# A one-core network kernel with routed experts: two indirect scatters in flight instead of one, and expert tiles of the first half that wait only for the first half's scatters and clears

## The chip, the cores and the metric

The kernel runs on one core of one Trainium2 chip. The metric is device time in microseconds (us), the median of a few executions. A profiled execution gives the trace: its span is the time between the first and the last instruction, its own time is a little longer. Engines are called PE (TensorE), DVE (VectorE), ACT (ScalarE), POOL (GpSimd) and SP (SyncE, used here only to issue DMAs).

## What is computed

Two layers on x of shape (4, 2048, 256) in float32, each sublayer with a layer norm ahead and a residual add behind:

```
x = x + L0_attn(norm(x))   # q, k, v projections, short convolution, gated delta rule (16 heads of 16), output projection
x = x + L0_ffn(norm(x))    # 32 experts, each token goes to 8 of them; plus a shared MLP
x = x + L1_attn(norm(x))   # state-space scan over the sequence, 16 states
x = x + L1_ffn(norm(x))    # rows quantized to a 6-bit grid in blocks of 32, then a 256 x 256 product
```

For the change the routed part of `L0_ffn` matters. For each of the 8192 tokens the gate picks 8 experts, and the token's normalized row (256 floats, 1 KB) goes through each of them; the results are summed with weights. That is 65536 routed rows.

## The kernel before

**Three stages.** The sequence is cut into NB = 16 blocks of 512 tokens (128 positions of each of 4 sequences). The first stage is a software pipeline over the blocks (`for j in range(-2, NB + 1)`), with parts called A (input norm, projections), B (the pair matrices of the delta rule and their solve), C (the sequential state update) and P (output projection, routing, shared MLP). P works on block p = j - 1. The second stage is the list of expert tiles; the third, mixed with the second half of the tiles, sums the expert rows per token and does layer 1.

**Halves.** Blocks 0 to 7 are half 0 and blocks 8 to 15 are half 1. Each half has its own DRAM scratch for routed rows (`xs[h]`, seen as scr_xs) and for expert outputs (`ys[h]`, seen as scr_ys). In `xs[h]` each expert owns a region; the rows of a token go to the next free places. `tables(h)` at the end of a half turns the counts into a tile list: NTH = 159 tiles of TILE = 256 rows for a half, NT = 318 in all.

**Scatter.** For block i, P leaves the normalized rows in `xn_r[:, i % 2]` (two buffers) and the destinations in `idx[:, i % 2]`. POOL then issues NC * TOPK = 4 * 8 = 32 indirect DMAs for the block, each of 128 rows of 1 KB. Before each it waits until the one before has landed, so one is under way at any time. There are two semaphores `s_scat`, one for even and one for odd blocks. ACT, before it writes `xn_r` for block p (`route_rows`, seen as line L890, output xn_r), waits until all scatters of block p - 2 have landed, because they read the same buffer.

**Clears.** A tile of 256 rows can reach past the rows that an expert has, so the 256 rows behind each expert's last row are set to zero: `clear_ends(h)` has SP read 32 positions from `ztab` and issue 32 DMAs of 256 KB from `zeros` (line L803). For half 0 this stands in SP's list behind the loads of j = 9; for half 1 behind everything that SP loads for the first stage. 64 more DMAs of fixed place (L795) run at the start; all 128 count on `s_zero`.

**Tiles.** `load_tile(t)` on SP reads a position and an expert number from the table, and issues the load of the rows into `xt` (6 buffers, L825) and of the expert's weights into `wr` (6 buffers, L832). PE transposes the tile (L618), computes gate and up (L629) and down (L637); ACT copies and applies Silu; DVE multiplies (L1721); ACT issues the store to scr_ys (L1116). Ahead of the first load SP waits:

```
sp.wait_ge(s_tab, HALVES)
sp.wait_ge(s_zero, 16 * 2 * HALVES * E)
for n in range(2):
    sp.wait_ge(s_scat[n], 16 * NC * TOPK * NB // 2)
```

that is, for the tables of both halves, all 128 clears and all 512 scatters. The order of work on each engine is written out by hand; each engine carries out its own list in order.

**Gather.** POOL goes on with 512 indirect DMAs that fetch expert rows into `yg` (L869), with two under way: one semaphore for each, used in turn. Those of a half wait until all tiles of that half are stored.

Of the kernel before, what the change touches and what calls it, by code (L numbers as in the profile page):

```python
# [9 lines left out]
NC = TB // CH  # L10
# [68 lines left out]
def network_kernel(nc, x, wproj, wo, wdelta, wb_state, wgate, wc_state, wshared, wexp, wquant, sel,  # L79
# [13 lines left out]
    with ExitStack() as ctx:  # L93
# [204 lines left out]
        s_zero = sem("s_zero")  # L298
        s_xt = [sem(f"s_xt{n}") for n in range(NX)]
# [23 lines left out]
        CHUNKS = NC * NB  # L323
        block = ctx.enter_context(nc.Block())
# [445 lines left out]
        def _(sp):  # L770
# [27 lines left out]
            def clear_ends(h):  # L798

                sp.wait_ge(s_ztab, h + 1)  # L800
                for e in range(E):
                    at = sp.value_load(ztab[0:1, h, e:e + 1], min_val=0, max_val=ROWS - TILE)
                    sp.dma_start(xs[h][bass.ds(at, TILE), :].rearrange("(p r) d -> p (r d)", r=2), zeros[:])\  # L803
                        .then_inc(s_zero, 16)
# [3 lines left out]
            for j in range(1, NB + 1):  # L808
                if j + 3 < NB:
                    load_x(j + 3)  # L810
                load_res(j)
                if j == HB + 1:
                    clear_ends(0)
            clear_ends(1)
            sp.wait_ge(s_tab, HALVES)
            sp.wait_ge(s_zero, 16 * 2 * HALVES * E)
            for n in range(2):
                sp.wait_ge(s_scat[n], 16 * NC * TOPK * NB // 2)
# [16 lines left out]
            for t in range(NT):  # L835
                load_tile(t)
            sp.wait_ge(s_store, 64 * NB)
# [3 lines left out]
        def _(pool):  # L841
            for i in range(NB):
                pool.wait_ge(s_idx, i + 1)
                for c in range(NC):
                    for k in range(TOPK):
                        sent = i // 2 * NC * TOPK + c * TOPK + k
                        if c or k:
                            pool.wait_ge(s_scat[i % 2], 16 * sent)
                        elif i:
                            pool.wait_ge(s_scat[(i - 1) % 2], 16 * ((i - 1) // 2 + 1) * NC * TOPK)  # L850
                        nc.gpsimd.indirect_dma_start(  # L851
                            xs[i // HB][:, :], bass.IndirectOffsetOnAxis(idx[:, i % 2, c, k:k + 1], 0),
                            xn_r[:, i % 2, c, :], None).then_inc(s_scat[i % 2], 16)
# [23 lines left out]
        def _(act):  # L877
# [20 lines left out]
            def route_rows(p):  # L898
                if p >= 2:
                    act.wait_ge(s_scat[p % 2], 16 * NC * TOPK * (p // 2))  # L900
# [1004 lines left out]
```

## Time and profile before

| | |
|---|---|
| median of 3 runs | 3666.69 us (3666.28 to 3671.66) |
| profiled execution, its own time | 3663.13 us |
| its span | 3661.3 us |
| mean granted TensorE clock | 0.825 |
| busy: PE, DVE, ACT, POOL | 2712.2, 2153.5, 1565.2, 1048.7 us |
| issues of indirect scatter (L851) | 512, from 328.5 to 1935.9 us |
| loads of tiles (L825, L832) | 318 each, the first at 1939.1 us |

Times in the rows are us from the start of the span. A row of the time line gives start, length, engine, line, operation, output and inputs, a count and, in brackets, how long the engine was idle before and what ended the idle time. For a DMA issue from POOL the length is the time in which POOL makes the transfer's descriptors, not that of the data. SPq is SP's queue.

### The profile page before, as it was taken

How to read it: one execution, taken by the hardware profiler on the slowest of the kernel's cores; microseconds unless marked ns; L12 is line 12 of the kernel's file. 1: busy time of each engine (PE TensorE's matmuls, PEld its weight loads, DVE VectorE, ACT ScalarE, POOL GpSimd, SP SyncE). 2: the span in 40 equal slices, each digit the busy share in tenths (PEclk: the TensorE clock that was granted, in tenths of full speed). 3: DMA queues.
4: the chain of work that ended last, by engine and by line, in shares of the span. 5: the costliest groups of instructions: out<-in, count | busy, mean ns of one | idle time of the engine just before them, and what ended most of it. 6: DMA issues, size and time to landing. Idle time of an engine off the chain costs nothing.

```text
span 3661.3 us, 109753 instructions
## 1 busy us (share of the span) xinstructions
PE 2712.2 (74%) x46188; PEld 2021.3 (55%) x46188; DVE 2153.5 (59%) x4702; ACT 1565.2 (43%) x2625; POOL 1048.7 (29%) x1028
## 2 busy tenths in 40 slices
PE   4578888888878887875207999997898888643544
PEld 2355555555555655554106888886777777422322
DVE  4878888888888888772201222213444444676675
ACT  4445555545544555511003444444555554432231
POOL 0001333333332333333330000014434431366661
PEclk8768788888888788766558999998999999876666
DMA  6001111111114111111317999997888887333331
GB/s 241 8 9 36 61 56 61 50 64 62 62 62 148 62 61 55 56 56 57 141 52 245 303 305 304 304 311 232 266 280 262 272 266 247 120 94 94 99 93 34
DMA packets 240349, 511.79 MB, mean 140 GB/s; under 512 B 38770, under 2 KB 63860, under 8 KB 239732
## 3 DMA queue, kind: packets, MB, share of 16 engines
q1 hardware_dynamic: 133396, 270.32, 22.6%
q0 software_dynamic: 49152, 134.28, 11.8%
q10 hardware_dynamic: 57312, 100.16, 7.5%
q8 instruction: 368, 6.03, 0.7%
q14 instruction: 121, 0.99, 0.1%
HBM read 303.82 MB, written 200.80 MB: 138 GB/s over the span
## 4 chain that ended last, share of the span: by engine, by line
DMA 55%; PE 28%; issue 7%; DVE 5%; ACT 3%; POOL 1%; SPq 0%; ACTq 0%; POOLq 0%; DVEq 0%
DMA scr_xs<-xn_r,idx 40%; DMA yg<-scr_ys,idx_y 14%; PE ps L629 13%; PE ps L637 6%; PE ps L618 3%; DVE tmp L1426 1%; DVE tu L1429 1%; PE ps L377 1%; DVE conv L1356 1%; PE ps L706 1%; PE ps L669 1%; DMA out<-x 1%; POOL yg L869 1%; PE ps L688 1%; PE ps L364 0%
## 5 line engine op out<-in xcount | busy, mean ns | idle before, releaser
L851 POOL DMA_INDIRECT scr_xs<-xn_r,idx x512 | 528.9, 1033 | 1407.5 <-DMA scr_xs<-xn_r,idx 1062.4
L869 POOL DMA_INDIRECT yg<-scr_ys,idx_y x512 | 519.7, 1015 | 1129.2 <-DMA scr_ys<-y 574.4
L1721 DVE TENSOR_TENSOR h<-sg,ps 128x256 f32<-128x256 f32 x318 | 133.1, 420 | 829.3 <-ACT sg L1106 790.6
L629 PE MATMUL ps<-xT,wr 128*128 128x256 f32 x2544 | 617.1, 386 | 0.0
L629 PEld LDWEIGHTS ps<-xT,wr 128*128 128x128 f32 x2544 | 470.5, 195 | 62.0 <-issue 8.6
L1748 DVE SCALAR_TENSOR_TENSOR x<-yg,wsel,x 128x256 f32<-128x256 f32 x512 | 247.8, 485 | 220.3 <-DMA yg<-scr_ys,idx_y 201.9
L637 PE MATMUL ps<-wr,h 128*128 128x256 f32 x1272 | 334.1, 386 | 57.8 <-DVE h L1721 31.5
L914 ACT ACTIVATE xT<-ps 128x512 f32<-128x512 f32 x382 | 225.3, 594 | 210.5 <-PE ps L618 173.2
L618 PE MATMUL ps<-identity,xt 128*128 128x128 f32 x1272 | 195.7, 277 | 149.9 <-DMA xt<-scr_xs 149.9
L637 PEld LDWEIGHTS ps<-wr,h 128*128 128x128 f32 x1272 | 242.9, 192 | 98.4 <-DVE h L1721 34.0
L914 ACT ACTIVATE y<-ps 128x512 f32<-128x512 f32 x318 | 189.8, 597 | 202.0 <-PE ps L637 186.8
L447 PE MATMUL ps<-sq,w_proj 128*128 128x512 f32 x512 | 271.7, 671 | 3.7 <-ACT raw L958 1.5
L1106 ACT ACTIVATE sg<-ps 128x256 f32<-128x256 f32 x318 | 122.0, 384 | 346.2 <-PE ps L629 322.8
L618 PEld LDWEIGHTS ps<-identity,xt 128*128 128x128 f32 x1272 | 162.4, 144 | 184.3 <-issue 149.4
L1429 DVE TENSOR_TENSOR tu<-tu,tmp 128x60 f32<-128x60 f32 (+14 forms) x480 | 242.9, 506 | 16.5
L377 PE MATMUL ps<-nq,kne 32*32 32x64 f32 x8192 | 197.6, 256 | 71.4 <-issue 40.5
L1426 DVE TENSOR_TENSOR tmp<-tu 128x60 f32<-128x60 f32 (+14 forms) x480 | 241.1, 502 | 13.4
L377 PEld LDWEIGHTS ps<-nq,kne 32*32 32x32 f32 x8192 | 171.4, 132 | 96.9 <-issue 72.8
L1356 DVE SCALAR_TENSOR_TENSOR conv<-raw,conv_w,conv 128x512 f32<-128x512 f32 x288 | 194.9, 744 | 16.0 <-ACT raw L958 16.0
L407 PEld LDWEIGHTS ps<-r_sb,tt 32*32 32x32 f32 x8192 | 135.5, 144 | 106.2 <-issue 72.3
L407 PE MATMUL ps<-r_sb,tt 32*32 32x16 f32 x8192 | 148.6, 207 | 53.9 <-issue 28.7
L393 PEld LDWEIGHTS ps<-s_sb,nq 32*32 32x32 f32 x8192 | 101.3, 118 | 127.7 <-issue 127.5
(244 smaller groups left out, 4216.8 us busy)
## 6 DMA issues: line engine op xcount, KB each, us to landing
wr<-in_wexp SPq DMA_DIRECT2D x318, 384.0 KB
xt<-scr_xs SPq DMA_DIRECT2D x318, 256.0 KB
scr_ys<-y ACTq DMA_DIRECT2D x318, 256.0 KB
scr_xs<-zeros SPq DMA_DIRECT2D x128, 256.0 KB
x_in<-in_x SPq DMA_DIRECT2D x64, 128.0 KB
x_res<-in_x SPq DMA_DIRECT2D x64, 128.0 KB
scr_xs<-xn_r,idx POOLq DMA_INDIRECT x512, 2.6
scr_x<-x_res SPq DMA_DIRECT2D x16, 512.0 KB
```

The costliest lines, as they stand in the source:

```text
L377: last = pe.matmul(ps[quad(q), AP + g, b * 128 + e * 64:b * 128 + e * 64 + 64], kne[quad(q), e, g, at], nq[quad(q), i % 2, :, g, at], star ...
L407: last = pe.matmul(ps[quad(q), RU, D + u * HD:D + (u + 1) * HD], tt[quad(q), c // 2, :, (c % 2) * H + u], r_sb[quad(q), u * HD:(u + 1) * H ...
L447: last = pe.matmul(ps[:, bank, :], w_proj[:, k, w, g * P:(g + 1) * P], xT[:, k, :], start=k == 0, stop=k == G - 1)
L618: last = pe.transpose(ps[:, bank, k * TILE + r * P:k * TILE + (r + 1) * P], xt[:, t % NX, r, k * P:(k + 1) * P], identity[:])
L629: last = pe.matmul(ps[:, bank, half * TILE:(half + 1) * TILE], wr[:, t % NW, at:at + EI], xT2[:, t % NH, k, :], start=k == 0, stop=k == G - 1)
L637: last = pe.matmul(ps[:, bank, r * D:(r + 1) * D], h2[:, t % NH, r * P:(r + 1) * P], wr[:, t % NW, 2 * G * EI:], start=True, stop=True)
L851: nc.gpsimd.indirect_dma_start(xs[i // HB][:, :], bass.IndirectOffsetOnAxis(idx[:, i % 2, c, k:k + 1], 0), xn_r[:, i % 2, c, :], None).the ...
L869: nc.gpsimd.indirect_dma_start(yg[:, n % NG, k, :], None, ys[h][:, :], bass.IndirectOffsetOnAxis(idx_y[:, i, c, k:k + 1], 0))\
L914: nc.scalar.activation(dst, src, func, **more).then_inc(s_xe[bank], 1)
L1426: sT.did(V.tensor_tensor(part, tu[:, :, j + 1:, j:j + 1].broadcast_to([P, 2, rows, j]), tu[:, :, j:j + 1, 0:j].broadcast_to([P, 2, rows, j ...
L1429: sT.did(V.tensor_tensor(tu[:, :, j + 1:, 0:j], tu[:, :, j + 1:, 0:j], part, ALU.add))
L1748: last = V.scalar_tensor_tensor(row, yg[:, n % NG, k, :], wsel[:, i, c, k:k + 1], row, ALU.mult, ALU.add)
```

## The change

Two things are edited. POOL's scatters use the two semaphores by turn within a block (k even or odd) instead of by block, and each scatter waits only for the last but one before it; ACT's wait ahead of `xn_r` still covers all scatters of block p - 2, now on both semaphores. And the clears behind the experts' rows count on a semaphore for each half, `s_ends`. SP's wait ahead of the first tile asks for the scatters of blocks 0 to 7 (SENT * HB on each semaphore) and the clears of half 0, the wait for all scatters and for the clears of half 1 stands ahead of tile 159, and the 32 clears of half 1 are issued one at a time, behind tiles 3, 7, ..., 127. The wait for both tables stays.

```diff
+        SENT = 16 * NC * TOPK // 2
...
-            def clear_ends(h):
-
+            def clear_end(h, e):
                 sp.wait_ge(s_ztab, h + 1)
-                for e in range(E):
-                    at = sp.value_load(ztab[0:1, h, e:e + 1], min_val=0, max_val=ROWS - TILE)
-                    sp.dma_start(xs[h][bass.ds(at, TILE), :].rearrange("(p r) d -> p (r d)", r=2), zeros[:])\
-                        .then_inc(s_zero, 16)
+                at = sp.value_load(ztab[0:1, h, e:e + 1], min_val=0, max_val=ROWS - TILE)
+                sp.dma_start(xs[h][bass.ds(at, TILE), :].rearrange("(p r) d -> p (r d)", r=2), zeros[:])\
+                    .then_inc(s_ends[h], 16)
...
                 if j == HB + 1:
-                    clear_ends(0)
-            clear_ends(1)
+                    for e in range(E):
+                        clear_end(0, e)
             sp.wait_ge(s_tab, HALVES)
-            sp.wait_ge(s_zero, 16 * 2 * HALVES * E)
+            sp.wait_ge(s_zero, 16 * HALVES * E)
+            sp.wait_ge(s_ends[0], 16 * E)
             for n in range(2):
-                sp.wait_ge(s_scat[n], 16 * NC * TOPK * NB // 2)
+                sp.wait_ge(s_scat[n], SENT * HB)
...
             for t in range(NT):
+                if t == NTH:
+                    sp.wait_ge(s_ends[1], 16 * E)
+                    for n in range(2):
+                        sp.wait_ge(s_scat[n], SENT * NB)
                 load_tile(t)
+                if t % 4 == 3 and t < 4 * E:
+                    clear_end(1, t // 4)
...
-                        sent = i // 2 * NC * TOPK + c * TOPK + k
-                        if c or k:
-                            pool.wait_ge(s_scat[i % 2], 16 * sent)
-                        elif i:
-                            pool.wait_ge(s_scat[(i - 1) % 2], 16 * ((i - 1) // 2 + 1) * NC * TOPK)
+                        way, turn = k % 2, (NC * i + c) * TOPK // 2 + k // 2
+                        if turn:
+                            pool.wait_ge(s_scat[way], 16 * turn)
                         nc.gpsimd.indirect_dma_start(
                             xs[i // HB][:, :], bass.IndirectOffsetOnAxis(idx[:, i % 2, c, k:k + 1], 0),
-                            xn_r[:, i % 2, c, :], None).then_inc(s_scat[i % 2], 16)
+                            xn_r[:, i % 2, c, :], None).then_inc(s_scat[way], 16)
...
                 if p >= 2:
-                    act.wait_ge(s_scat[p % 2], 16 * NC * TOPK * (p // 2))
+                    for way in range(2):
+                        act.wait_ge(s_scat[way], SENT * (p - 1))
```

POOL's list at the first block reads so before (ztab, idx, tab are the tables named above; a count behind a row is of equal rows):

```order
L851 DMA scr_xs<-xn_r,idx 147456x256 [waits s_idx]
L851 DMA scr_xs<-xn_r,idx 147456x256 [waits s_scat0] x31
L851 DMA scr_xs<-xn_r,idx 147456x256 [waits s_scat0,s_idx]
L851 DMA scr_xs<-xn_r,idx 147456x256 [waits s_scat1] x31
L851 DMA scr_xs<-xn_r,idx 147456x256 [waits s_scat1,s_idx]
```

and the same place in the changed kernel:

```order
L856 DMA scr_xs<-xn_r,idx 147456x256 [waits s_idx]
L856 DMA scr_xs<-xn_r,idx 147456x256
L856 DMA scr_xs<-xn_r,idx 147456x256 [waits s_scat0]
L856 DMA scr_xs<-xn_r,idx 147456x256 [waits s_scat1]
L856 DMA scr_xs<-xn_r,idx 147456x256 [waits s_scat0]
L856 DMA scr_xs<-xn_r,idx 147456x256 [waits s_scat1]
```

The number and the order of the scatters are the same; the second has no wait any more, and each later one waits for its own semaphore only.

SP's list between the last store of the first stage (L783) and the first tile load reads so before, with the first and the last of 32 clears:

```order
L783 DMA scr_x<-x_res 128x1024 [waits s_x1]
L802 TENSOR_LOAD ztab [waits s_ztab,s_x1st]
L802 ISA x2
L803 ISA
L803 DMA scr_xs<-zeros 128x512
...
L803 DMA scr_xs<-zeros 128x512
L822 TENSOR_LOAD tab [waits s_scat0,s_scat1,s_zero,s_tab]
L822 ISA x2
L825 ISA
L825 DMA xt<-scr_xs 128x512
```

and so in the changed kernel:

```order
L785 DMA scr_x<-x_res 128x1024 [waits s_x1]
L823 TENSOR_LOAD tab [waits s_ends0,s_scat0,s_zero,s_scat1,s_tab,s_x1st]
L823 ISA x2
L826 ISA
L826 DMA xt<-scr_xs 128x512
L830 TENSOR_LOAD tab
L830 ISA x2
L833 ISA
L833 DMA wr<-in_wexp 128x768
```

The 32 clears are gone from this place. Behind the weights of tile 3 one of them now stands ahead of the rows of tile 4, in SP's list of the changed kernel:

```order
L833 DMA wr<-in_wexp 128x768
L802 TENSOR_LOAD ztab [waits s_ztab]
L802 ISA x2
L803 ISA
L803 DMA scr_xs<-zeros 128x512
L823 TENSOR_LOAD tab
L823 ISA x2
L826 ISA
L826 DMA xt<-scr_xs 128x512
```

The same piece of four rows comes behind every fourth tile up to tile 127.

## Rows read from the trace of the kernel before

**Rows 1.** The page: chain that ended last by share, and the costliest group of POOL.

```profile
DMA 55%; PE 28%; issue 7%; DVE 5%; ACT 3%; POOL 1%; SPq 0%; ACTq 0%; POOLq 0%; DVEq 0%
DMA scr_xs<-xn_r,idx 40%; DMA yg<-scr_ys,idx_y 14%; PE ps L629 13%; PE ps L637 6%; PE ps L618 3%; DVE tmp L1426 1%; DVE tu L1429 1%; PE ps L377 1%; DVE conv L1356 1%; PE ps L706 1%; PE ps L669 1%; DMA out<-x 1%; POOL yg L869 1%; PE ps L688 1%; PE ps L364 0%
L851 POOL DMA_INDIRECT scr_xs<-xn_r,idx x512 | 528.9, 1033 | 1407.5 <-DMA scr_xs<-xn_r,idx 1062.4
```

**Rows 2.** Stretches: length, busy by engine with counts, granted clock, DMA share, GB/s.

```profile
core 0: us, PE busy (x) PEld busy (x) DVE busy (x) ACT busy (x) POOL busy (x), PEclk, DMA share, GB/s
900.00:1000.00 100.00, 82.61 (x2591) 58.07 (x2580) 88.48 (x199) 53.01 (x80) 33.01 (x32) 0.85 0.19 60
1800.00:1900.00 100.00, 0.00 (x0) 0.00 (x0) 0.00 (x0) 0.00 (x0) 34.50 (x36) 0.50 0.32 117
2000.00:2400.00 400.00, 400.00 (x2115) 352.56 (x2114) 107.33 (x189) 193.95 (x396) 0.00 (x0) 1.00 0.93 304
```

**Rows 3.** Time line, first and last scatter, last table, SP's clears, first tile.

```profile
328.54 1.83 POOL L851 DMA_INDIRECT scr_xs<-xn_r,idx  x1 [328.08 <-DVE wsel L1562]
1793.89 36.32 SPq L803 DMA_DIRECT2D scr_xs<-zeros  x32
1794.33 0.28 DVE L1614 CAST tab<-ps 8x128 int32<-8x128 f32 x1 [0.47 <-PE ps L515]
1935.89 0.96 POOL L851 DMA_INDIRECT scr_xs<-xn_r,idx  x1 [1.71 <-DMA scr_xs<-xn_r,idx]
1939.09 0.37 SPq L825 DMA_DIRECT2D xt<-scr_xs  x1
```

**Rows 4.** The chain around 1785 us: start, length, what.

```profile
1785.49 2.40 DMA scr_xs<-xn_r,idx
1787.88 0.27 issue
1788.15 2.41 DMA scr_xs<-xn_r,idx
```

**Rows 5.** ACT's waits from 1250 to 1800 us: total, times, longest.

```profile
ACT xn_r L890 <- DMA scr_xs<-xn_r,idx: 67.7, 6, 27.7
```

**Rows 6.** Time line of ACT and DVE, the last two of these waits.

```profile
1662.34 2.07 ACT L890 ACTIVATE xn_r<-x_res,off_route,std_route 128x256 f32<-128x256 f32 x4 [22.34 <-DMA scr_xs<-xn_r,idx]
1760.72 2.07 ACT L890 ACTIVATE xn_r<-x_res,off_route,std_route 128x256 f32<-128x256 f32 x4 [27.67 <-DMA scr_xs<-xn_r,idx]
1771.02 0.69 DVE L1567 TENSOR_TENSOR h_s<-sq_o,ps 128x512 f32<-128x512 f32 x1 [37.79 <-PE ps L487]
```

**Rows 7.** Time line of DVE, last routing step of blocks 1, 7, 9 and 12.

```profile
428.04 1.22 DVE L1562 TENSOR_REDUCE wsel<-sq_o 128x32 f32<-128x1024 f32 x1
1017.02 1.22 DVE L1562 TENSOR_REDUCE wsel<-sq_o 128x32 f32<-128x1024 f32 x1
1223.62 1.22 DVE L1562 TENSOR_REDUCE wsel<-sq_o 128x32 f32<-128x1024 f32 x1
1534.98 1.22 DVE L1562 TENSOR_REDUCE wsel<-sq_o 128x32 f32<-128x1024 f32 x1
```

**Rows 8.** Stretches again, columns as in rows 2.

```profile
2440.00:2460.00 20.00, 20.00 (x108) 17.64 (x107) 2.43 (x6) 9.90 (x20) 5.71 (x6) 1.00 0.99 346
3200.00:3300.00 100.00, 46.58 (x280) 29.18 (x280) 70.16 (x140) 31.86 (x52) 61.20 (x57) 0.71 0.32 96
```

**Rows 9.** Time line of POOL, first and 25th gather.

```profile
2442.68 0.97 POOL L869 DMA_INDIRECT yg<-scr_ys,idx_y  x1 [505.83 <-DMA scr_ys<-y]
2499.35 0.94 POOL L869 DMA_INDIRECT yg<-scr_ys,idx_y  x1 [1.95 <-DMA yg<-scr_ys,idx_y]
```

**Rows 10.** The chain in the tile stage, one tile and the start of the next.

```profile
2100.16 0.44 PE ps L618 x4
2100.60 1.73 PE ps L629 x8
2102.33 0.86 PE ps L637 x4
2103.19 0.44 PE ps L618 x4
```

More of the change, by code:

```diff
@@ L298, in network_kernel @@
         s_zero = sem("s_zero")
+        s_ends = [sem(f"s_ends{h}") for h in range(HALVES)]
         s_xt = [sem(f"s_xt{n}") for n in range(NX)]
```

## The prediction

> **What bounds the kernel now.** I read the chain of work that ended last first. Its shares say where to look: 40% of the span are landings of the indirect scatters, and they are one costly group, 512 issues with 1062.4 us of POOL's idle time ended by the scatter before [rows 1]. So POOL is not busy: it waits for its own last transfer. The chain's pieces show one turn of this: 2.40 us from issue to landing and 0.27 us to the next issue, 2.67 us for a scatter when nothing else runs [rows 4]. From the first issue at 328.54 to the last at 1935.89 there are 511 steps, 3.15 us each [rows 3]; while DVE and PE are busy a turn is longer, 32 in a stretch of 100 us [rows 2].
>
> Next I read the stretches. From 900 to 1000 us the first stage works at full load (DVE 88%, PE 83%), from 1800 to 1900 nothing but POOL works, and from 2000 to 2400 PE is busy all the time at the full clock, with a DMA share of 0.93 [rows 2]. So there are three limits in a row: the first stage at DVE's and PE's own pace, a gap that is scatters alone, and tiles at PE's pace. A tile takes PE 3.03 us, from 2100.16 to 2103.19, without a gap [rows 10].
>
> Two places show what the scatters cost. One is the gap: the last table is written at 1794.61 (1794.33 and 0.28), and the first tile load goes out at 1939.09 [rows 3]. The last scatter lands at about 1938.3 (1935.89 and the 2.40 of [rows 4]), so SP needs 0.8 us after its last wait ends. The other is inside the first stage: ACT waits six times, 67.7 us in total, for scatters of two blocks before, the last two times 22.3 and 27.7 us [rows 5, 6].
>
> **The change part by part.** (1) The gap. The first tile now asks for the tables, the scatters of blocks 0 to 7 and the clears of half 0. All but the second table are long done at 1794: by blocks of 32 turns of about 3.15 us, block 7 has landed at about 1140. So the table ends the wait, and the first load goes out at 1794.61 + 0.8 = 1795.4 on the old clock, against 1939.09: **143.7 us** gained. The 32 clears that stood here took SP 36.3 us [rows 3]; they are hidden now by scatters that go on for another 108 us, and would have delayed the first tile by some 35 us had they stayed, but they are moved away.
>
> (2) The first stage. With two under way a turn is at best half of 2.67 us, 1.33, and not less than POOL's own 1.03 [rows 1, 4]. The trace has no pair of scatters. The nearest rows are the gathers, the same kind of transfer the other way, two at a time: 57 in 100 us beside a busy DVE, 1.75 us each [rows 8]; and beside a DMA load at its limit 24 turns from 2442.68 to 2499.35, 2.36 us each [rows 9]. Upper bound 3.15 (no help at all). I take 1.9, as DVE is busier here. A block of 32 then takes 61 us. The blocks come 98.2 us apart where ACT doesn't stall (428.04 to 1017.02, six blocks [rows 7]), so the backlog is gone and ACT's waits with it. Up to what pace does this hold? 98.2 / 32 = 3.07 us, far above 2.36.
>
> What are the 67.7 us worth? Blocks 9 to 12 come in 311.4 us [rows 7], and three times 98.2 is 294.6: 16.8 us late, and the waits in them are about what is left when the last two (50.0) are taken off the 67.7, that is 17.7. So the early waits pass on in full. The last two fall where A and B have run out; DVE then sits idle 37.8 us for the step that follows the wait [rows 6], so they pass on too. A part of each wait, some 0.4 us, is DVE's step that ends together with it: 67.7 - 6 x 0.4 = **65 us** gained. Bounds: 0 if pairs don't help; 50 if only the last two pass on; 68 at most.
>
> (3) The tile stage of half 0 gets new load. SP issues 32 clears more, 1.135 us each (36.32 / 32, [rows 3]), one for four tiles. Of four tiles' 12.1 us SP's eight issues take, at that same length, 9.1, and the ninth makes 10.2: SP keeps up. Behind a clear stand the rows of the next tile, later by 1.1 us; with six buffers they are asked for some tiles ahead, and PE waits for nothing there today [rows 2]. The DMA engines get 32 x 256 KB = 8.4 MB of clears over 128 tiles (388 us, 22 GB/s) and, at the start, the last block's scatters, 4.2 MB. At 2.2 us a turn these are 70 us with 60 GB/s. Demand is 304 + 22 + 60 = 386 GB/s for 70 us, then 326. From below: from 2440 to 2460, with gathers in pairs beside the tiles, the engines carried 346 GB/s at a share of 0.99 and PE was busy 20.00 of 20.00 us [rows 8]. So 326 costs nothing, and 386 is 40 over: 2.8 MB, 8 us, if the scatters keep their pace; they need not, since each waits for the last but one and so slows down under load; in those 20 us six gathers went out, 3.3 us a turn. I take **4 us** lost. From above: if 304 GB/s were all there is for this mix, 12.6 MB are 41 us.
>
> The Trainium skill ("SBUF — State Buffer", the bandwidth table in "A bandwidth-pool intuition that's wrong") gives about 358 GB/s between HBM and one core. By it the overload of 28 GB/s for 70 us would be 2.0 MB, 5.5 us, and the sum 1.5 us worse than mine; the 346 GB/s in [rows 8] agree with it as far as they go.
>
> (4) The rest. The wait ahead of tile 159 comes some 480 us after the first load; the last scatter has landed within 32 x 2.4 = 77 us and the last clear stands behind tile 127. POOL's gathers wait for the tiles of half 0, not for the scatters. From tile 0 on, the rest of the program is the old one, moved earlier.
>
> **Sum.** 143.7 + 65 - 4 = 205 us. The profiled execution took 3663.1 (span 3661.3 and 1.8 around it): 3458. The median of the runs, 3666.7, is 3.6 above it, so I predict **3462**.
>
> **The rivals.** *Transfers bound the first half of the tiles.* The share is 0.93 already and 9% of bytes (12.6 MB to 159 tiles of 896 KB, 146 MB) are added in that stage. For it: 0.93 at 304 GB/s; against it: 346 GB/s with PE full. Price 41 in place of 4: 3499. The Trainium skill ("DMA: Bandwidth & Descriptors", "Queues, rings and completion order") says that each DMA engine serves its queue rows in turn, packet by packet, so scatters would take their turns from tile loads however late those are; it speaks for this rival, and no stretch shown has scatters beside tiles.
>
> *The first stage doesn't get faster.* Pairs of scatters are held up by each other or by DVE (POOL's step is 1033 ns in the mean against 960 when alone [rows 1, 3]), so that the pace stays above 3.07; or another wait takes over. Then only the gap is gained: 143.7 - 4, which is 3527. Against it: the gathers' 1.75 and 2.36.
>
> *Slower than before.* Two scatters in flight disturb each other so much that the first stage is held back. ACT's last wait, for block 15, ends when blocks 0 to 13 are out, 448 turns after 328.54; it is at 1760.72 now. It eats the whole 143.7 us at (1760.72 + 143.7 - 328.54) / 448 = 3.52 us a turn, 7.0 us for one scatter with another beside it; at 3.7 us a turn the time is 81 us longer, 3748. A gather in a pair takes 4.7 us at the DMA engines' limit, so nothing shown comes near it.
>
> **How the numbers follow.** Chances: the forecast 0.72, with a range of its own from 3443 to 3485 (first stage 50 to 75 with a little of the clock, tiles 0 to 12); transfers 0.12; no gain in the first stage 0.13; slower 0.03. The range of 8 in 10 takes in the first and most of the second: 3440 to 3508; the third and fourth are left out. What can be told from no change is 0.2%, 7 us. All cases but the last are faster by far more: faster 0.96, same 0.01, slower 0.03.
>
> **What would show it.** In the changed kernel's time line the first tile load is within 1 to 2 us of the last table, which is written at about 1730; ACT's wait for scatters ahead of xn_r is gone from the list of waits; scatters take 1.5 to 2.3 us a turn, and come in bursts of about 60 us with pauses. In the stretches the idle 100 us are gone, and the first half's tiles take PE 3.03 us each, 159 of them in about 487 us, a few more if transfers bind. I am wrong if the turn stays above 3 us, if PE waits for xt or wr in tiles 0 to 158, or if the first stage keeps its length with ACT's waits gone.

## The result, and the profile after

The changed kernel took **3822.37 us** (median of 4 runs, 3806.79 to 3825.7), the kernel before in the same session 3669.18 (3666.28 to 3673.98). The ratio is 1.0408 [1.0376, 1.044]: 4% slower, where I forecast 5.6% faster and gave slower a chance of 0.03. The profiled execution took 3806.79 us, span 3804.8, mean granted clock 0.814.

The time line of the changed kernel, with the rows that answer to [rows 3, 7, 9] (last routing step of blocks 1, 7, 12 and 15, last table, first tile, first gather):

```profile
445.12 1.22 DVE L1568 TENSOR_REDUCE wsel<-sq_o 128x32 f32<-128x1024 f32 x1
1191.21 1.22 DVE L1568 TENSOR_REDUCE wsel<-sq_o 128x32 f32<-128x1024 f32 x1
1812.44 1.22 DVE L1568 TENSOR_REDUCE wsel<-sq_o 128x32 f32<-128x1024 f32 x1
2072.75 1.22 DVE L1568 TENSOR_REDUCE wsel<-sq_o 128x32 f32<-128x1024 f32 x1
2079.00 0.28 DVE L1620 CAST tab<-ps 8x128 int32<-8x128 f32 x1 [0.37 <-PE ps L517]
2080.13 0.37 SPq L826 DMA_DIRECT2D xt<-scr_xs  x1
2589.27 0.98 POOL L874 DMA_INDIRECT yg<-scr_ys,idx_y  x1 [433.48 <-DMA scr_ys<-y]
```

The gap is gone: the first tile goes out 0.85 us behind the last table. But the last table is 284.7 us later than in [rows 3], and the whole first stage is slower from its start: blocks 1 to 7 come 124.3 us apart ((1191.21 - 445.12) / 6), against 98.2 in [rows 7]. From first tile load to first gather it is 509.1 us, 5.5 more than in [rows 3, 9]. The sum: -143.7 (gap) + 284.7 + 5.5 leaves 146.5; the profiled executions differ by 143.7, so the rest of the program gave back 3.

The stretches of the changed kernel, columns as in [rows 2]; the first is the time in which POOL issues block 6's scatters, the second the pause until block 7's, the third is tiles:

```profile
1070.00:1122.00 52.00, 27.56 (x652) 19.82 (x652) 21.48 (x38) 11.64 (x19) 32.51 (x32) 0.59 0.34 113
1122.00:1190.00 68.00, 58.06 (x1762) 37.40 (x1763) 60.59 (x153) 36.37 (x56) 0.00 (x0) 0.85 0.02 4
2100.00:2500.00 400.00, 396.75 (x2083) 345.97 (x2082) 106.36 (x186) 192.57 (x390) 19.47 (x20) 1.00 0.98 328
```

This is where the time goes. While POOL issues, PE carries out 652 matmuls in 52 us, 12.5 per us; in the pause 1762 in 68, 25.9 per us. Before, it was 25.9 per us with scatters spread over the whole block [rows 2]. DVE falls with PE, 38 instructions against 153. The DMA engines have room, at a share of 0.34. The lower clock, 0.59, comes with PE's idle time. It can't make the loss: PE is busy for only 27.56 of these 52 us, slow matmuls included, and the gaps between matmuls are "issue" (below), in which the engine waits for nothing that the profile shows.

The list of waits of the changed kernel (total us, times, longest), and under it one row of the kernel before:

```profile
POOL scr_xs L856 <- DVE wsel L1568: 1321.6, 16, 323.7
DVE a_c L1413 <- PE ps L379: 273.9, 43, 31.8
PEld ps L379 <- issue: 266.9, 347, 7.3
POOL scr_xs L856 <- DMA scr_xs<-xn_r,idx: 252.7, 298, 4.0
PE ps L379 <- issue: 166.6, 303, 3.4
DVE a_c L1413 <- remote: 139.9, 15, 28.0
```

```profile
DVE a_c L1407 <- PE ps L377: 127.2, 56, 5.2
```

ACT's wait for scatters of [rows 5] is gone, as foretold, and POOL waits for new work in place of its own transfer. DVE's wait for `a_c`, the masked pair matrices, has grown from 127.2 us, never over 5.2 at once, to 273.9 + 139.9 ("remote" stands where the trace shows no releaser; the instruction is the same), with up to 31.8 at once. PE makes these matrices from very many small matmuls (L379). Their group on the page, and POOL's, to set beside [rows 1]:

```profile
L856 POOL DMA_INDIRECT scr_xs<-xn_r,idx x512 | 511.2, 998 | 1644.1 <-DVE wsel L1568 1321.6
L379 PE MATMUL ps<-nq,kne 32*32 32x64 f32 x8192 | 292.0, 274 | 214.2 <-issue 166.6
```

The time line shows what "issue" looks like. PE in the first stretch, POOL at the same time, and the first full batch of PE behind the last scatter:

```profile
1106.83 0.45 PE L379 MATMUL ps<-nq,kne 32*32 32x64 f32 x6 [0.32 <-issue]
1107.58 0.45 PE L379 MATMUL ps<-nq,kne 32*32 32x64 f32 x6 [0.31 <-issue]
1108.34 0.44 PE L379 MATMUL ps<-nq,kne 32*32 32x64 f32 x5 [0.31 <-issue]
1109.10 0.42 PE L379 MATMUL ps<-nq,kne 32*32 32x64 f32 x4 [0.32 <-issue]
1109.85 0.45 PE L379 MATMUL ps<-nq,kne 32*32 32x64 f32 x5 [0.33 <-issue]
1111.29 0.46 PE L379 MATMUL ps<-nq,kne 32*32 32x64 f32 x6 [1.00 <-issue]
...
1125.77 2.71 PE L379 MATMUL ps<-nq,kne 32*32 32x64 f32 x128
```

```profile
1106.72 0.96 POOL L856 DMA_INDIRECT scr_xs<-xn_r,idx  x1 [0.30 <-issue]
1108.11 0.96 POOL L856 DMA_INDIRECT scr_xs<-xn_r,idx  x1 [0.42 <-DMA scr_xs<-xn_r,idx]
1109.39 0.96 POOL L856 DMA_INDIRECT scr_xs<-xn_r,idx  x1 [0.32 <-DMA scr_xs<-xn_r,idx]
```

Beside scatters 1.3 to 1.4 us apart PE gets 26 small matmuls in 3.47 us, 7.5 per us, in handfuls 0.76 us apart. Without them 128 take 2.71 us, 47 per us. I call this the hold: PE's small matmuls are held up while POOL makes descriptors. It doesn't look like the fetch of blocks of instructions. The instruction queue's row among the DMA queues, in the first stretch and in the second (packets, MB, share), is

```profile
q8 instruction: 5, 0.08, 0.7%
...
q8 instruction: 14, 0.23, 1.4%
```

5 and 14 packets of 16 KB are in proportion to what PE carried out (1304 and 3525 matmuls and weight loads, some 250 to 260 a packet), and a late one would be expected to show as one pause in so many instructions, not as handfuls of five. That is argued from the counts; no run was made for it. The Trainium skill ("Runtime: NRT & Kernel Launch", "Instruction fetch mechanics") puts such a block at 256 instructions, which agrees with the packets: 5 x 256 = 1280 for the 1304 matmuls and weight loads of that stretch.

### The profile page after: what moved, and what is told of

Read it like the earlier page. It is cut to its first block, busy times and chain, and to the rows that moved or that the text cites. A ratio compares the mean times of both kernels' runs of the same rounds, so it can differ in the third digit from the quotient of the medians.

```text
span 3804.8 us, 109754 instructions
## 1 busy us (share of the span) xinstructions
PE 2790.6 (73%) x46188; PEld 2060.5 (54%) x46188; DVE 2151.1 (57%) x4702; ACT 1566.6 (41%) x2625; POOL 1036.3 (27%) x1028
## 4 chain that ended last, share of the span: by engine, by line
PE 38%; DVE 25%; DMA 15%; issue 13%; ACT 3%; SPq 2%; another core or an unknown queue 2%; POOL 1%; ACTq 0%; DVEq 0%; POOLq 0%
DMA yg<-scr_ys,idx_y 13%; PE ps L631 10%; PE ps L379 6%; DVE tmp L1432 6%; PE ps L639 5%; DVE tu L1435 5%; DVE conv L1362 4%; PE ps L620 3%; PE ps L409 2%; PE ps L465 2%; PE ps L500 1%; PE ps L395 1%; PE ps L366 1%; DMA xt<-scr_xs 1%
## 5 line engine op out<-in xcount | busy, mean ns | idle before, releaser
L856 POOL DMA_INDIRECT scr_xs<-xn_r,idx x512 | 511.2, 998 | 1644.1 <-DVE wsel L1568 1321.6
L379 PE MATMUL ps<-nq,kne 32*32 32x64 f32 x8192 | 292.0, 274 | 214.2 <-issue 166.6
L379 PEld LDWEIGHTS ps<-nq,kne 32*32 32x32 f32 x8192 | 214.3, 141 | 290.6 <-issue 266.9
L1413 DVE TENSOR_TENSOR a_c<-ps,m_strict 128x512 f32<-128x512 f32 x64 | 66.1, 1034 | 421.1 <-PE ps L379 273.9
L449 PE MATMUL ps<-sq,w_proj 128*128 128x512 f32 x512 | 248.9, 623 | 2.9 <-ACT raw L964 1.5
L395 PE MATMUL ps<-s_sb,nq 32*32 32x32 f32 x8192 | 125.2, 211 | 105.3 <-issue 63.5
```

The source lines that it names most:

```text
L379: last = pe.matmul(ps[quad(q), AP + g, b * 128 + e * 64:b * 128 + e * 64 + 64], kne[quad(q), e, g, at], nq[quad(q), i % 2, :, g, at], star ...
L449: last = pe.matmul(ps[:, bank, :], w_proj[:, k, w, g * P:(g + 1) * P], xT[:, k, :], start=k == 0, stop=k == G - 1)
L856: nc.gpsimd.indirect_dma_start(xs[i // HB][:, :], bass.IndirectOffsetOnAxis(idx[:, i % 2, c, k:k + 1], 0), xn_r[:, i % 2, c, :], None).the ...
```

## The experiments

The first session looked for the cause in the program: which part of the change, and then whether descriptors or bytes. Theory D came after it. The number of the chip stands with each session.

### First session (chip 11; the kernel before 3704.62 us, 3695.29 to 3712.55)

**Pairs alone.** Tile wait and clears as before:

```diff
+            for e in range(E):
+                clear_end(1, e)
...
-            sp.wait_ge(s_ends[0], 16 * E)
-            for n in range(2):
-                sp.wait_ge(s_scat[n], SENT * HB)
+            for h in range(HALVES):
+                sp.wait_ge(s_ends[h], 16 * E)
+            for n in range(2):
+                sp.wait_ge(s_scat[n], SENT * NB)
...
```

The wait ahead of tile 159 and the clears inside the list of tiles are taken out with it.

> The changed kernel's scatters (two in flight), but the old order around the tiles: all 32 clears of half 1 and the wait for all 512 scatters stand ahead of the first tile. Theory A: the making of a scatter's descriptors on POOL holds up PE's small instructions (in both traces PE starts 3 to 5 times fewer of them in the microsecond after an issue), and with two in flight these holds come one behind the other in a burst of 50 us, in which the first stage runs at half pace. Then the first stage is as long as in the changed kernel: 122 us a block, last table at about 2079 us, and the gap is 45 us (32 scatters at 1.45): about 3860 us. Theory B: the slow first stage comes from the other part of the change (clears and waits on SP, the longer wait list on ACT). Then the first stage takes 98 us a block or less, with no stall of ACT, the last table stands at about 1730 and the first tile at about 1780: about 3510 us.

Measured: **3457.8 us** (3449.82 to 3460.16), ratio 0.9334 [0.9313, 0.9355]. Pairs made the kernel 6.7% faster.

**Early tiles alone**, one scatter under way:

```diff
-                        if turn:
-                            pool.wait_ge(s_scat[way], 16 * turn)
+                        if turn or k:
+                            pool.wait_ge(s_scat[1 - way], 16 * (turn + way))
```

> The changed kernel with each scatter waiting for the one just before it (on the other of the two semaphores), so one in flight as before; tiles and clears as in the changed kernel. Theory A: first stage as before the change (98 us a block, last table at about 1795), first tile load 0.9 us behind the table, and the tile stage of half 0 some 6 us longer than before (in the changed kernel it was 5.6 us longer from first load to first gather): 3669 - 144 + 6, about 3531 us. Theory B: the first stage stays at 122 us a block, about 3820 us.

Measured: **3556.29 us** (3554.55 to 3559.16), ratio 0.9597 [0.9575, 0.962].

**No scatters** (POOL's loop over the 512 scatters and all waits for them taken out), and **half rows**:

```diff
-                            xs[i // HB][:, :], bass.IndirectOffsetOnAxis(idx[:, i % 2, c, k:k + 1], 0),
-                            xn_r[:, i % 2, c, :], None).then_inc(s_scat[way], 16)
+                            half[i // HB][:, :], bass.IndirectOffsetOnAxis(idx[:, i % 2, c, k:k + 1], 0),
+                            xn_r[:, i % 2, c, 0:D // 2], None).then_inc(s_scat[way], 16)
```

> No scatters at all: the 512 indirect DMAs and every wait for them are left out, and the tiles read a place of the scratch that holds zeros, so the output is another one and only the first stage is to be read. It shows what the first stage costs with nothing from POOL. Theory A: even single scatters cost PE something (its rate after an issue falls in the kernel before too), so a block takes less than the 98 us of before: 85 to 95. If single scatters cost nothing, it is 98 again, with the last table at about 1730 since ACT has no stall.

> Two scatters in flight as in the changed kernel, but each moves half of a row (512 bytes) into a scratch of its own, 128 rows as before; tiles read zeros, so the output is another one and only the first stage is to be read. As many descriptors, half the bytes. Theory A (descriptor making holds PE up): 118 to 123 us a block, as in the changed kernel. Theory C (the data of two scatters crowd the DMA engines or the memory that PE reads): the excess over 98 us halves, about 110 us a block or less.

Measured, one run each: 3395.75 us without scatters, 3417.09 with half rows. Without any scatter blocks came about 95 us apart, with the pairs alone 95.9. The routing steps of blocks 1, 7 and 15 in the pairs alone:

```profile
417.47 1.22 DVE L1565 TENSOR_REDUCE wsel<-sq_o 128x32 f32<-128x1024 f32 x1
992.70 1.22 DVE L1565 TENSOR_REDUCE wsel<-sq_o 128x32 f32<-128x1024 f32 x1
1682.93 1.22 DVE L1565 TENSOR_REDUCE wsel<-sq_o 128x32 f32<-128x1024 f32 x1
```

Neither theory fits both parts: for the pairs alone A wanted 3860 us and B 3510, for the early tiles alone A wanted 3531 and B 3820. Here the scatters cost the first stage next to nothing (1 us a block), and neither part of the change is slow by itself. Two theories were left: A', that pairs and early tiles are slow only together, since the changed kernel as a whole did not run on chip 11, and D, that some chips hold PE up while POOL makes descriptors and others do not.

### Second session (chip 15; the kernel before 3669.03 us, 3659.42 to 3675.38)

Three programs already known, unedited: the changed one, the one before, and the pairs alone.

> The changed kernel once more, unedited, now beside the kernel before and the pairs-only kernel in one job. Theory D: what slowed the first stage is not in the program but in where the first measurement ran: there PE started 3 to 5 times fewer small instructions in the microsecond in which POOL makes descriptors, in the kernel before too, and in the four runs of the second job it did not. Then, where that hold is absent, the changed kernel takes 3458 (pairs only) less the gap of about 46 us and plus 6 for the fuller tile stage: about 3415 us, a ratio of 0.92 to before; where it is present, about 3820 again. Theory A', the rest of theory A: the clears and the early tiles together with the pairs slow the first stage wherever it runs: 3820 us here too, with pairs-only at 3458.

> The kernel before, unedited, for its trace in this job. Theory D: if before is near 3705 us here as in the second job, PE's rate does not fall in the microsecond after a scatter's issue, though it did in the first trace of before, and a scatter takes longer in turn (3.2 us or more). If before is near 3669, the fall is there again.

> The pairs-only kernel again, for its trace beside the changed kernel's in the same job. Theory D: its first stage has the same pace as the changed kernel's, slow (122 us a block) or fast (95 us a block) together. Theory A': 95 us a block here, 122 in the changed kernel.

Measured: changed **3785.14** (3773.51 to 3798.82), ratio 1.0312 [1.0284, 1.0341]; before 3680.15 (one run); pairs alone **3788.19** (one run), its blocks 1, 7 and 15 at

```profile
440.90 1.22 DVE L1565 TENSOR_REDUCE wsel<-sq_o 128x32 f32<-128x1024 f32 x1
1155.15 1.22 DVE L1565 TENSOR_REDUCE wsel<-sq_o 128x32 f32<-128x1024 f32 x1
2015.98 1.22 DVE L1565 TENSOR_REDUCE wsel<-sq_o 128x32 f32<-128x1024 f32 x1
```

The same program, the same instructions: 119.0 us a block here, 95.9 on chip 11, and 330 us in the whole. D held and A' fell: the pairs alone are as slow here as the changed kernel. The choice of chip explains both sessions.

### Third session (chip 10; the kernel before 3701.02 us, 3688.34 to 3708.7)

The changed kernel again, the early tiles alone, the kernel without scatters, and a new one in which POOL clears a small row four times behind each scatter of blocks 0 to 13:

```diff
+                        if i < NB - 2:
+                            for n in range(4):
+                                nc.gpsimd.memset(idle[:], 0.0).then_inc(s_idle, 1)
+                                pool.wait_ge(s_idle, 4 * (NC * TOPK * i + c * TOPK + k) + n + 1)
```

> The changed kernel once more, as the yardstick for the three kernels beside it. It tells whether this chip holds PE up while POOL makes descriptors. With the hold (D): blocks about 121 us apart, 3780 to 3825 us, the kernel before near 3669. Without it: blocks about 96 us apart and 3415 us, that is the 3458 of the pairs alone on such a chip less about 45 us for the early first tile, the kernel before near 3705. A theory in which the change itself is bad for the first stage on every chip wants 3780 or more in both cases.

> The changed kernel, but for blocks 0 to 13 POOL clears a small row four times behind each scatter, which takes time and nothing else, so that a turn is 2.2 to 3.0 us in place of 1.4 to 1.8, with two scatters still allowed under way. If the loss comes from how densely descriptors are made (D), a hold of 1 us in 2.6 us leaves PE as much room as in the kernel before: on a chip with the hold blocks come 98 to 103 us apart and the time is 3460 to 3510. If it comes from the amount of descriptors (as many in a block), blocks stay 115 us or more apart and the time above 3700. If two transfers under way are the cause (rival), it lies between, near 3700. On a chip without the hold all three want about 3420 us.

> One scatter under way, early tiles. With the hold: the old first stage and the gap's gain alone, 3669 - 144 + 6 = 3531 us, blocks 98 us apart. Without the hold about 3556 us as measured on such a chip. If one under way were not what keeps the first stage whole, blocks would be near 120 us apart and the time about 3760.

> Leaves the scatters and the waits for them out, the tiles read rows of zeros. If POOL's scatters are what slows the first stage (D), blocks come 94 to 96 us apart on either kind of chip, and the time is about 3396 us as on the chip without the hold. If the chip's PE is slow by itself where the hold was seen (rival), blocks stay 110 to 120 us apart and the time is above 3650.

Measured: changed **3415.23** (3408.87 to 3420.17), ratio 0.9237 [0.9204, 0.927]; paced 3426.8 (3421.47 to 3430.92), 0.9269 [0.9238, 0.93]; early tiles alone 3561.63 (3546.36 to 3573.79), 0.9634 [0.9588, 0.9681]; without scatters 3399.02 (3394.33 to 3403.71). The chip was without the hold, the number expected for the changed kernel was 3415, and nothing was told apart about the hold. The time line of the changed kernel here, PE and then POOL in a burst:

```profile
916.92 3.20 PE L379 MATMUL ps<-nq,kne 32*32 32x64 f32 x110 [1.98 <-issue]
```

```profile
916.85 0.96 POOL L856 DMA_INDIRECT scr_xs<-xn_r,idx  x1 [1.22 <-DMA scr_xs<-xn_r,idx]
918.12 0.96 POOL L856 DMA_INDIRECT scr_xs<-xn_r,idx  x1 [0.30 <-issue]
```

110 small matmuls in 3.20 us without a gap, while POOL makes the descriptors of two scatters; batches of this same line drip in handfuls in the first trace. (The pause of 1.98 us ahead of them is of another kind: the kernel without any scatter has such ones too, up to 2.3 us long.) Two stretches, a burst and then tiles:

```profile
901.00:957.00 56.00, 47.17 (x1476) 33.72 (x1476) 46.86 (x86) 26.48 (x45) 33.17 (x32) 0.88 0.32 104
1782.00:2182.00 400.00, 399.27 (x2106) 350.89 (x2105) 99.97 (x182) 193.74 (x396) 0.00 (x0) 1.00 0.95 321
```

26.4 matmuls per us inside the burst, against 12.5 in the first trace.

### Fourth session (chip 6; the kernel before 3699.93 us, 3696.46 to 3708.82)

> The paced kernel again, for a chip with the hold (the kernel before near 3669). If the density of descriptor making is what costs (D), one hold in 2.9 us leaves PE as much room as in the kernel before (3.1 to 3.3 us a turn): blocks 98 to 103 us apart, and 3460 to 3510 us. If the number of descriptors is what costs, blocks stay 115 us or more apart and the time is above 3700. If it is that two transfers are under way (rival), also near 3700, at 2.9 us a turn. On a chip without the hold it is 3427 us as before, and nothing is told apart.

> No scatters and no waits for them, the tiles read rows of zeros. On a chip with the hold, D expects blocks 94 to 96 us apart and about 3398 us, as on the others. If PE is slow there by itself (rival): blocks 110 to 120 us apart, above 3650 us.

> The changed kernel with rows of 512 bytes in place of 1 KB, written to a scratch of its own; the tiles read rows of zeros. As many descriptors, half the bytes. If making descriptors holds PE up (D), the stage is as slow as with whole rows on a chip with the hold: blocks 117 to 125 us apart, about 3780 us. If it is the transfers' bytes, the excess halves: blocks near 108 us apart, about 3600 us. On a chip without the hold it is 3417 us as before.

Measured: 3424.03 (3417.49 to 3430.21), 3389.67 and 3407.14 us. Again no hold, so none of the three says what it was meant for.

### Fifth session (chip 7; the kernel before 3663.38 us, one run)

As the chip can't be chosen, one kernel carries six kinds of scatter, a few blocks of each. `live(n)` counts the blocks before n that scatter at all, in place of n in the waits. The tiles read rows of zeros, and blocks 7, 8, 11 and 12 aren't scattered at all:

```diff
+    MODE = ("two",) * 3 + ("half",) * 2 + ("paced",) * 2 + ("clear",) * 2 + ("one",) * 2 + ("none",) * 2 + ("two",) * 3
...
+                        if MODE[i] == "one":
+                            pool.wait_ge(s_scat[1 - way], 16 * (turn + way))
+                        elif turn and MODE[i] in ("two", "half", "paced"):
+                            pool.wait_ge(s_scat[way], 16 * turn)
...
```

> The changed kernel with a kind of scatter that changes from block to block: 0 to 2 in pairs as in the changed kernel, 3 and 4 pairs with rows of 512 bytes, 5 and 6 pairs with four small clears by POOL behind each (2.9 us a turn), 7 and 8 no scatters but the same clears, 9 and 10 one scatter under way, 11 and 12 nothing at all, 13 to 15 pairs. The tiles read rows of zeros. On a chip with the hold (blocks 0 to 2 about 121 us apart): D, the density of descriptor making, wants 115 to 125 for half rows, 95 to 103 for the paced pairs, 94 to 96 for clears only and for nothing, 98 to 103 for one under way. The bytes as the cause want about 108 for half rows; two under way as the cause 115 or more for the paced pairs; a PE slow by itself about 120 everywhere; POOL's activity of any kind 100 or more in the blocks with clears only. On a chip without the hold all blocks up to 12 are 94 to 98 apart (103 at block 8) and nothing is told apart.

Measured: 3568.56 us (one execution), on a chip with the hold. The distance of the routing steps of block i and i + 1, in which block i's scatters go out, beside the changed kernel on chip 10:

| block i | kind | us to the next, chip 7 | changed kernel, chip 10 |
|---|---|---|---|
| 0, 1, 2 | pairs | 122.2, 109.9, 124.1 | 95.4, 97.6, 94.9 |
| 3, 4 | pairs, half rows | 123.5, 129.2 | 98.7, 95.9 |
| 5, 6 | pairs, paced | 93.6, 97.6 | 94.1, 95.2 |
| 7, 8 | clears only | 101.4, 96.0 | 103.3, 97.6 |
| 9, 10 | one under way | 99.1, 98.0 | 97.3, 95.8 |
| 11, 12 | nothing | 94.7, 85.5 | 93.4, 82.3 |
| 13, 14 | pairs | 91.7, 50.8 | 67.0, 49.9 |

The stretches of blocks 2 (pairs), 4 (half rows), 5 (paced), 10 (one) and 11 (nothing) of this kernel:

```profile
554.70:678.80 124.10, 88.62 (x2429) 56.83 (x2428) 84.05 (x191) 51.05 (x78) 31.89 (x32) 0.78 0.15 49
802.30:931.50 129.20, 88.08 (x2440) 59.67 (x2440) 84.30 (x192) 51.03 (x78) 32.03 (x32) 0.78 0.10 31
931.50:1025.10 93.60, 75.40 (x2421) 51.95 (x2421) 84.57 (x192) 51.82 (x78) 73.01 (x158) 0.93 0.20 64
1419.20:1517.20 98.00, 80.96 (x2430) 55.72 (x2430) 84.46 (x192) 49.75 (x77) 31.19 (x32) 0.87 0.19 62
1517.20:1611.90 94.70, 78.89 (x2443) 55.30 (x2441) 84.31 (x192) 53.13 (x80) 3.91 (x4) 0.89 0.06 20
```

Each stretch holds the same work (2421 to 2443 matmuls, DVE 84.1 to 84.6 us), and the half rows are as slow as whole ones at the lowest traffic of all that scatter, 31 GB/s. So it isn't bytes. The paced pairs move 64 GB/s and lose nothing, so it isn't the number of descriptors either, which is the same 32 x 128 in all of them. What is left is how densely they are made, or that two scatters are under way. The paced pairs alone don't tell these two apart. Two are allowed in them, but a scatter lands 2.4 us after its issue at the earliest and 2.8 us in the median of block 5, so in blocks 5 and 6 only 20 of the 58 turns whose landing the trace shows had one still under way when the next went out. DVE's wait in the same stretches of pairs, half rows and paced pairs:

```profile
DVE a_c L1434 <- remote: 30.0, 1, 30.0
...
DVE a_c L1434 <- PE ps L387: 39.7, 3, 32.4
...
DVE a_c L1434 <- PE ps L387: 5.4, 2, 3.0
```

One wait of 30 to 32 us is the whole excess of each of these two blocks of pairs and half rows. (Block 1, at 109.9 us, had waits of 15.9 us for a_c and a smaller excess; why it lost less stays open.) The row of the time line that belongs to the middle one: from 829.43 to 852.73 us PE gets 36 of a batch of 128 small matmuls, then

```profile
852.73 2.78 PE L387 MATMUL ps<-nq,kne 32*32 32x64 f32 x92 [0.44 <-issue]
```

The half rows' last scatter goes out at 848.43, 4.3 us ahead of this row, so the hold outlasts the making of a burst's descriptors by some 3 us. It even outlasts the transfers: the last packet of the scatters ends at 850.33, and their last landing is at 850.6, 2.1 us ahead of the row.

**One scatter alone holds PE too.** The kernel before has never two under way, and its first trace shows the hold behind a single issue, PE and then POOL:

```profile
351.81 1.54 PE L377 MATMUL ps<-nq,kne 32*32 32x64 f32 x95
353.49 0.32 PE L377 MATMUL ps<-nq,kne 32*32 32x64 f32 x5 [0.15 <-issue]
354.24 0.59 PE L377 MATMUL ps<-nq,kne 32*32 32x64 f32 x26 [0.42 <-issue]
```

```profile
352.93 0.96 POOL L851 DMA_INDIRECT scr_xs<-xn_r,idx  x1 [1.93 <-DMA scr_xs<-xn_r,idx]
```

From 353.35 to 354.24 PE gets 5 matmuls, before and after it runs freely. Counted over whole traces (blocks 0 to 12, or those named), PE starts so many small (32x32) weight loads per us behind a scatter's issue:

| trace | 0 to 0.8 us | 0.8 to 1.2 us | 1.4 to 2.2 us |
|---|---|---|---|
| kernel before, first measurement | 14.6 | 7.3 | 36.3 |
| kernel before, chip 15 | 14.9 | 8.3 | 35.0 |
| mixed, one under way (9, 10), chip 7 | 17.6 | 6.1 | 36.1 |
| mixed, paced pairs (5, 6), chip 7 | 15.5 | 4.6 | 40.9 |
| early tiles alone (one under way), chip 10 | 25.3 | 27.6 | 21.2 |

So a second transfer isn't needed for the hold. It lasts some 1.2 us behind a lone issue, about as long as the making of the descriptors (0.96 to 1.1 us) and a good deal shorter than the 2.4 us and more to the landing. With 2.9 us a turn each hold is followed by some 1.7 us of free run, and DVE waits only 5.4 us for a_c in block 5. With 1.3 to 1.6 us a turn nearly nothing but hold is left, and the batch takes as long as the burst lasts. That density alone makes the loss, and two scatters under way add nothing to it, fits all of this; a dense burst with never two under way was not run.

### Last three sessions (chips 13, 14, 12; the kernel before 3702.41, 3697.7, 3696.04 us)

The paced kernel, to time it as a whole where there is a hold.

> The paced kernel on a chip with the hold, if this is one (the kernel before near 3669). By the mixed kernel's distances, 94 to 98 us for blocks with paced pairs, the first stage is as on the other chips but for block 14, whose scatters go out unpaced: last table at about 1700 to 1720, first tile 1 us later, and 3425 to 3450 us in all, against 3785 to 3822 for the changed kernel and 3669 for the one before. If something in the whole kernel undoes it, blocks 100 us or more apart and above 3480. On a chip without the hold 3427 us as before, and the kernel before near 3700.

> The paced kernel, one more try to meet a chip with the hold (the kernel before near 3669, not 3700). There 3425 to 3450 us, blocks 0 to 13 94 to 98 us apart, by the mixed kernel's distances; blocks 100 us or more apart and above 3480 if something in the whole kernel undoes it. On a chip without the hold 3425 us, as three times before.

> The paced kernel, the last try. On a chip with the hold (the kernel before near 3669) 3425 to 3450 us with blocks 94 to 98 us apart; above 3480 us if something in the whole kernel undoes it. On a chip without the hold 3414 to 3427 us, as four times before.

Measured: 3422.13 (3418.66 to 3432.57), ratio 0.925 [0.9206, 0.9295]; 3414.39 (3412.64 to 3418.34), 0.9234 [0.9207, 0.9262]; 3421.22 (3413.18 to 3426.75), 0.9262 [0.9212, 0.9312]. All three chips were without the hold. On such chips the paced kernel is within 12 us of the changed one; as a whole it has not been timed on one with the hold, so that it beats both kernels there (some 3440 us, an estimate from the distances of the table, with block 14's scatters unpaced) is argued and not shown.

## Why the prediction was wrong

**Step (1), the gap, was right.** 0.85 us from table to first tile against 0.8, and all 143.7 us. The early tiles alone gave 3701.0 - 3561.6 = 139.4 us on chip 10 and 148.3 on chip 11; steps (1) and (3) together said 139.7. How long the gap is in the kernel before on those two chips isn't known, as no trace of it was taken there, so these two sums agree with the steps and don't prove them one by one.

**Step (2), the first stage, failed.** It has two halves. That a block of 32 takes some 61 us, "so the backlog is gone and ACT's waits with it", was right: 1.6 us a turn at 1070 to 1122, and the waits gone. What failed is the sentence that held the rest up without saying so, that the blocks come 98.2 us apart whatever the scatters do. I took 98.2 as the stage's own pace from a trace in which descriptors are made once in 3.15 us, and asked only whether the scatters keep up with the stage, never what a denser POOL does to the stage. It became 124.3: some 26 us a block, 284.7 in all in place of -65. What the runs showed in its place: on such a chip each scatter's issue holds PE's small matmuls up for some 1.2 us, so that at 1.6 us a turn PE does 12.5 matmuls per us in place of 25.9 and DVE waits for it.

**The rival on the other side had the right sign and the wrong mechanism.** It looked for transfers that slow each other to over 3.52 us a turn. The pace was 1.4 to 1.8 in blocks 0 to 14, and it was the fast pace that hurt: on chip 7, 1.4 to 1.7 us a turn gave 110 to 129 us a block (0 to 4), and 2.9 gave 94 to 98. "If the first stage keeps its length with ACT's waits gone" stood among the signs of a wrong prediction; it is the one that came, and more.

**Step (3), tiles, was right**: 5.5 us against 4. The stretch of tiles, in which POOL issues the last 20 scatters, shows 328 GB/s (326 foretold, behind the scatters) at a share of 0.98 and PE busy 396.75 of 400 us, against 400.00 before. The transfers hardly bind, though they are near it.

**Step (4) was right** within 3 us.

**Where no hold is**, the gain was 286 us on chip 10 (3701.0 to 3415.2), more than the 205 of my sum. There the pairs gave 146.4 (3561.6 to 3415.2) in place of 65. With one under way ACT's waits were longer there,

```profile
ACT xn_r L895 <- DMA scr_xs<-xn_r,idx: 102.2, 6, 29.9
```

and blocks 3 to 11, 99 to 112 us apart, came down to 93 to 103, as the old pace of 3.2 to 3.4 us a turn lies above 3.07. So my size for (2) was too small there as well. The 102.2 don't make up 146.4, and the rest isn't accounted for. Nor is the 65 firm on a chip with the hold: a second trace of the kernel before, on chip 15, has 95.7 us of these waits in place of 67.7.

## What to carry to other kernels

The pace of a stage is measured beside what the other engines did at the time. Before making an engine issue its transfers faster, ask what else its issuing slows, and look for work of another engine that goes out in very many small instructions, where "issue" ends the idle time. Spreading descriptors evenly over a block (here 2.9 us a turn) kept the gain within 12 us on chips without the hold, and in the mixed kernel it kept blocks at 94 to 98 us on one with it. A change worth 7 to 8% on one chip and -3 to -4% on another should be timed on several before it is kept.

## What the runs showed of the hardware

- **Chips of one kind differ in this.** On chips 15 and 7, and on the one of the first measurement, whose kernel before takes 3663 to 3669 us, PE's 32x32 matmuls are held up while POOL makes descriptors. On chips 11, 10, 6, 13, 14 and 12, where it takes 3696 to 3705, the pairs alone, the changed kernel or the paced one shows none of it. The kernel before is some 30 to 40 us faster on chips with the hold, and no run says why. The same program with pairs alone takes 3788 on one and 3458 on another. What differs between them stays open, as does whether a chip is always of one kind: none of the numbered chips was met in two sessions, and the number of the first measurement's isn't known.
- **The hold has a rhythm**: four to six matmuls every 0.72 to 0.76 us, or one every 0.7 to 2 us late in a burst, while the DMA engines are at a third of their time. How one engine comes to slow another's issue was not tried, nor whether it is the making of the descriptors alone or also what the DMA engines do with them; clears by POOL alone don't do it (96.0 us, block 8).
- **A rival that no run touches is the recording of the trace.** Where the hold is dense, records are lost. Every scatter should leave 16 marks of its landing, 8192 in a trace; the changed kernel's first trace has 3575 of them and the pairs alone on chip 15 have 3591, but the changed kernel on chip 10 has 7936 and the kernel before 8192 on both of its traced chips. (Of the engines' own semaphore marks the same program has 8374 on the first chip and 8979 on chip 10, which may be why "remote" stands for a releaser above.) The hold outlasts the last landing by 2 us, as if something were still being worked off. Each execution here comes with a recorded span and clock, so none is known to have run unrecorded; whether the hold is there without any recording stays open.
- The Trainium skill ("SBUF — State Buffer", "SBUF: two separate sides") has PE on ports of its own that wait on nobody, and knows contention of POOL's descriptors with DVE alone. The hold, 7.5 against 47 matmuls per us, is not of that sort, though no run shows that a port is behind it; on chips without it the page's rule fits, 110 matmuls in 3.20 us beside two scatters.
- **Pairs of scatters** take 1.4 to 2.0 us a turn, against 3.0 to 3.6 for one under way in the same stage, and 2.9 where POOL clears four small rows (301 ns each) between them. One under way beside tiles takes 4.3 to 5.5 us a turn, in the early tiles alone.
